# Three output projections of a four-layer kernel turned round: weights stationary, 256 tokens moving, then a copy and two transposes

## What is computed

```
L0_attn:  16 query heads of 64, rotary, causal;    out = o[tokens, 1024] @ Wo[1024, 128]
L1_attn:  16 query heads of 64, normalised q, k, mixed down to 8 x 64;  out = o[tokens, 512] @ Wout[512, 128]
L2_xattn: 16 heads of 64 over the 257 context rows; out = sum over heads h of  u_h[tokens, 128] @ M_h[128, 128]
```

## Time and profile before

| | |
|---|---|
| median of 3 runs | 7036.16 us (7031.7 to 7041.08) |
| span of the profiled execution, first to last instruction | 6974.0 us |
| median less span | 62.2 us |
| mean granted TensorE clock | 0.740 of 2.4 GHz |
| PE matmul busy | 5171.6 us (74%), 32012 records |
| PE weight load busy | 3702.6 us (53%) |
| DVE busy | 3139.9 us (45%) |
| ACT busy | 1901.3 us (27%) |

### The profile page before, as it was taken

How to read it: one execution, slowest core, us unless ns; L and a number is a source line. 1 busy time by engine, 2 the same in 40 slices (tenths; PEclk the granted TensorE clock), 3 DMA queues, 4 the chain that set the end, 5 groups by cost and what they waited for, 6 DMA issues and landing times.

```text
span 6974.0 us, 94942 instructions
## 1 busy us (share of the span) xinstructions
PE 5171.6 (74%) x32012; PEld 3702.6 (53%) x32012; DVE 3139.9 (45%) x8375; ACT 1901.3 (27%) x5099; POOL 660.4 (9%) x438
## 2 busy tenths in 40 slices
PE   6868687686876868768786686866778668786777
PEld 4545555465554655545554465544655446554455
DVE  3545335453444534445344543445434454444543
ACT  3223132232322323223132231422323223232231
POOL 1101011010200102001020010200102000020000
PEclk7758687696866968668686686867868578685777
DMA  3000000001000010000100001000000000000000
GB/s 116 1 1 1 32 10 1 1 1 37 4 1 1 1 37 5 1 1 1 37 4 1 1 1 39 3 1 1 13 27 3 1 1 13 27 3 1 1 1 2
DMA packets 17466, 74.76 MB, mean 11 GB/s; under 512 B 2106, under 2 KB 10298, under 8 KB 10436
## 3 DMA queue, kind: packets, MB, share of 16 engines
q1 hardware_dynamic: 16964, 68.29, 3.0%
HBM read 66.18 MB, written 2.10 MB: 10 GB/s over the span
## 4 chain that ended last, share of the span: by engine, by line
issue 82%; POOL 9%; PE 6%; DVE 2%; ACT 1%; POOLq 0%; DVEq 0%; ACTq 0%
POOL own L1196 3%; POOL big L1196 2%; POOL odd L1213 2%; POOL mid L1196 2%; POOL own L1201 1%; PE dveb L401 1%; PE actb L863 1%; PE oddb L873 0%; PE evenb L554 0%; PE dveb L704 0%; PE evenb L685 0%; PE oddb L554 0%; PE evenb L608 0%; PE oddb L677 0%; PE evenb L654 0%
## 5 line engine op out<-in xcount | busy, mean ns | idle before, releaser
L1196 POOL TENSOR_TENSOR own<-own,rinv 128x1028 f32<-128x1028 f32 x128 | 243.4, 1901 | 3045.0 <-DVE rinv L1665 3045.0
L935 ACT ACTIVATE lnv<-mv,wts 128x2 f32<-128x2 f32 x257 | 75.9, 295 | 1487.6 <-DVE mv L1348 1445.7
L393 PE MATMUL actb<-wts,xn 128*128 128x128 f32 x418 | 118.3, 385 | 474.9 <-DVE xn L1354 228.0
L942 ACT ACTIVATE PT<-actb 128x512 f32<-128x512 f32 (+2 forms) x576 | 314.1, 578 | 455.2 <-PE actb L642 151.2
L685 PE MATMUL evenb<-ctxT,big 128*128 128x257 f32 x1024 | 286.8, 404 | 127.2 <-ACT own L1098 115.2
L1098 ACT ACTIVATE own<-evenb,nmax 128x257 f32<-128x257 f32 x512 | 239.3, 473 | 424.6 <-DVE nmax L1651 424.6
L393 PEld LDWEIGHTS actb<-wts,xn 128*128 128x128 f32 x418 | 59.3, 188 | 531.4 <-issue 478.3
L1453 DVE CUSTOM_DVE_ANT_0 big<-evenb,own 128x257 f32<-128x257 f32 x512 | 198.8, 421 | 304.3 <-issue 303.7
L704 PE MATMUL dveb<-PT,ctx 128*128 128x512 f32 x512 | 263.8, 640 | 60.2 <-ACT PT L942 60.2
L685 PEld LDWEIGHTS evenb<-ctxT,big 128*128 128x128 f32 x1024 | 180.3, 196 | 234.8 <-ACT own L1098 166.5
L436 PE MATMUL evenb<-big 32*128 32x257 f32 x1024 | 237.4, 500 | 59.1 <-DVE nmax L1453 43.3
(11 more groups left out here) (350 smaller groups left out, 11639.1 us busy)
## 6 DMA issues: line engine op xcount, KB each, us to landing
ctxT<-in_ctxT SPq DMA_DIRECT2D x16, 1032.0 KB, 4.6
own<-in_fside SPq DMA_DIRECT2D x64, 257.0 KB, 7.8
ctx<-in_ctx SPq DMA_DIRECT2D x16, 1024.0 KB, 6.8
wts<-in_weights SPq DMA_DIRECT2D x1, 10592.0 KB
big<-in_fold SPq DMA_DIRECT2D x1, 2048.0 KB, 8.6
x<-in_x SPq DMA_DIRECT2D x16, 128.0 KB, 2.4
out<-xn SPq DMA_DIRECT2D x16, 128.0 KB, 1.9
mid<-in_ints SPq DMA_DIRECT2D x1, 576.0 KB
```

The source lines that it names most:

```text
L393: last = transpose(ps[:, 128 * t:128 * t + 128], xn[s][:, t, :], ident)
L942: op = activation(dst, ps[0:parts, 0:n], func or ACT.Copy, scale=scale)
L1196: nc.gpsimd.tensor_tensor(P[:, :, 0:SK], P[:, :, 0:SK], rinv[0][:, :].unsqueeze(2).to_broadcast((128, 4, SK)), ALU.mult).then_inc(*p_ready ...
```

## The change

The projections of a0, a1 and x2 go through `project_swapped`: weights stationary, all 256 tokens moving, one bank of aR with the output feature-major. ACT copies it to `oT[s]`; in a new stage `tokens_out` PE transposes the two halves back into a bank of dR, and DVE adds it as before. `STAGES` grows by one for `a0o`, `a1o` and `x2`.

```
-        STAGES = dict(... a0o=3, ... a1o=4, ... x2=2 * NB + 4, ...)
+        STAGES = dict(... a0o=4, ... a1o=5, ... x2=2 * NB + 5, ...)
...
+                def project_swapped(weights, tokens):
+                    ps = bank(aR, "yT")
+                    for j in range(len(weights)):
+                        last = mm(ps[:, 0:TOK], weights[j], tokens[j], start=(j == 0), stop=(j == len(weights) - 1))
+                    last.then_inc(*aR.filled.done)
+
+                def tokens_out():
+                    have(aR, "yT")
+                    ps = bank(dR, "out")
+                    for t in range(TG):
+                        last = transpose(ps[:, 128 * t:128 * t + 128], oT[s][:, 128 * t:128 * t + 128], ident)
+                    last.then_inc(*dR.filled.done)
...
-                    project_out([a0_o[:, j, :] for j in range(8)], [w("a0_Wo")[:, 128 * j:128 * j + 128] for j in range(8)])
+                    project_swapped([w("a0_Wo")[:, 128 * j:128 * j + 128] for j in range(8)], [a0_o[:, j, :] for j in range(8)])
+                    yield
+                    tokens_out()
...
-                    project_out([a1_o[:, j, :] for j in range(4)], [w("a1_Wout")[:, 128 * j:128 * j + 128] for j in range(4)])
+                    project_swapped([w("a1_Wout")[:, 128 * j:128 * j + 128] for j in range(4)], [a1_o[:, j, :] for j in range(4)])
+                    yield
+                    tokens_out()
...
-                    project_out([x2_q[:, :, h] for h in range(H)], [MU[:, 1, h, :] for h in range(H)])
+                    project_swapped([MU[:, 1, h, :] for h in range(H)], [x2_q[:, :, h] for h in range(H)])
+                    yield
+                    tokens_out()
...
+                    drain(oT[s][:, :], TOK)          # ACT: in a0o, a1o and x2, in the stage of the projection
+                    yield
...
+                    yield                            # DVE: add_out one stage later
                     add_out()
```

More of the change, by code:

```diff
@@ L47 @@
     xn_ready0=13, xn_ready1=13, s_ready0=5, s_ready1=5, e_ready0=6, e_ready1=6, p_ready0=21, p_ready1=21,
-    mix_ready0=10, mix_ready1=10, act_bank_filled=208, act_bank_drained=208, dve_bank_filled=160,
+    mix_ready0=10, mix_ready1=10, act_bank_filled=214, act_bank_drained=214, dve_bank_filled=160,
     dve_bank_drained=160, even_bank_filled=164, even_bank_drained=164, odd_bank_filled=68, odd_bank_drained=68)
@@ L276, in four_layers @@
             flags += [r.filled, r.drained]
-        STAGES = dict(ln=3, ln1x=3, ln1a=4, ln3a=4, x0=NB + 4, a0p=4, a0o=3, f0=4, x1p=3, x1o=3, a1p=3 * TG + 3, a1o=4, f1=2 + 2 * TG,
-                      x2=2 * NB + 4, a2=6, f2=2, x3=6, a3p=3, a3o=7, f3=3 + TG)
+        STAGES = dict(ln=3, ln1x=3, ln1a=4, ln3a=4, x0=NB + 4, a0p=4, a0o=4, f0=4, x1p=3, x1o=3, a1p=3 * TG + 3, a1o=5, f1=2 + 2 * TG,
+                      x2=2 * NB + 5, a2=6, f2=2, x3=6, a3p=3, a3o=7, f3=3 + TG)
         SUBLAYERS = [["ln", "x0"], ["ln", "a0p", "a0o"], ["ln", "f0"], ["ln1x", "x1p", "x1o"], ["ln1a", "a1p", "a1o"], ["ln", "f1"],
@@ L1081, in a1o @@
                     yield
+                    drain(oT[s][:, :], TOK)
+                    yield
                 def f1():
```

## The result

| | before | changed |
|---|---|---|
| median | 7033.93 us (7029.5 to 7041.08, 4 runs) | 7079.84 us (7077.05 to 7087.58, 4 runs) |
| ratio | | 1.0072 (1.0051 to 1.0092), 46 us slower |
| profiled span, clock | 6974.0 us, 0.740 | 7077.8 us, 0.737 |

The two profiled spans differ by 103.8 us and the medians by 46. That gap has to be understood before any step is judged. The changed kernel's profiled execution took 7079.61 us: only 1.8 us lie outside its span. So the 62.2 us between the median and the span of before weren't launch and ends. The profiled execution of before was itself some 60 us shorter than the timed ones.

A forecast was written before the change was run, and what follows sets the result against it. One chain hopping between engines in a merged order bounds the kernel. Steps sum to +8.2 us a trip, +66 us over 8 trips, on 7036.2: 7102, said as 7100 us; range for 8 in 10, 6985 to 7165.

The forecast's parts named there:

- The pace of the strided operand: x2 projection: strided moving columns pay as strided weights did, 13.8 us for 14.05, a gain of 0.25 us.
- the middle bound: x2 projection: moving operand read at the strided weights' 1.72 ns per column, about 13.8 us, between 6.9 and 27.5.
- The first rival: x2 projection: strided moving columns cost nothing extra, 6.9 us for 13.8, 110 us less, 6992 us; chance 0.16.
- the second: x2 projection: stride paid twice per column, 27.5 us, 219 us more, 7320 us; chance 0.08.
- The third: Projection as forecast, but the new order worth as much as it costs, -2 us a trip, 7020 us; chance 0.11.
- Step 7: End with x2 before the a2 projection: wait for DVE, then transposes, x2 addition later; +1.3 us a trip.
- Step 6: f1.5 after the x2 projection adds 4.6 us, f1.4 and f1.2 moves save 4.8; 0 a trip, -3 to +4.
- Step 5: a1 projection before f1.5, +3.0 us; farther up a1p.4 earlier, f1.2 and softmax waiting, +1.2; +4.2 a trip.
- Step 4: a1 projection waits for its input's eviction, two transposes, a1o.1 delays x1o.1; +2.2 us a trip.
- Step 2: f0.3 stands behind the a0 projection, so its matmuls and DVE work delay the addition; +1.5 us a trip.
- 0 saved: a0 and a1 projections: half the records, twice as wide, no matmul time saved; at most 0.4 us each.
- Step 1: Values of a0 fill PE's wait for POOL, a0's addition waits for DVE; -1 us a trip, -3 to +2.

The follow-up runs named there:

- e6: Changed kernel's stage order, projections in the old form without copy or transposes, each addition in its projection's stage; against before: 7078.88 us, 1.0060.
- e4: All three projections turned round, copy and transposes in the projection's own stage, old stage order; against before: 7002.82 us, 0.9957.
- e10: Changed kernel's stage order, projections in the old form, each in the last stage right before its addition; against before: 7036.71 us, 1.0079.
- e1: Only the x2 projection turned round, with its extra stage, a0 and a1 as before; against before: 7001.91 us, 0.9956.

## Why the prediction was right, point by point

**The pace of the strided operand: right.** 0.431 us per record forecast, 0.43 measured. The gain was forecast at 0.25 us; from the first record's start to the last one's end the projection of step 7 went from 14.24 to 14.05 us, that of step 6 from 14.03 to 14.14. The choice of the middle bound rested on ACT's drain paying as the weights did, and the layouts confirm that reading. The first rival fell on this, and the second. The third, an order worth as much as it costs, fell on steps 1, 5 and 6, none of which came out at its lower end.

**Step 7: tail right, +1.4 against +1.3.** The step as a whole grew by 0.2 to 0.3 only: in the fourth trip DVE's last combination now starts 63.5 us into the step where it was 64.6. The stages ahead of it moved too, which the sum had left out; which of them gains the 1.1 us isn't shown.

**Step 6: near, -0.8 against 0.** The tail grew from 15.6 (631.62 - 616.04) to 20.5 us (640.99 - 620.50), +4.9 against +4.6 forecast, so the gain ahead of it was 5.7 against 4.8.

**Step 5: the tail right (+3.3 against +3.0), the front too small (+3.3 against +1.2).** The mechanism that was named, that a1p.8 loses the cover of f1.3, is what the traces show. The term that was mis-sized is the value taken from its bounds of -3 to +4: it was drawn to the middle by the earlier L1571. That operation does start 6.3 us earlier (30.8 us into the step against 37.1), but DVE's f1.2, now behind the scores of a1, starts 4.5 us later (50.0 against 45.5), the reciprocal 2.4 us later, and at the end of the softmax, 66.1 us into the step, the two kernels are level, with f1.3 done before the change and still to do after it.

**Step 4: right in size, +1.9 against +2.2.** But the order without the turned-round form gives +0.3 in e6, and the form without the order +0.3 in e4. In e10 the step takes 95.6 us in one kind of trip and 97.8 in the other, with the same instructions, so the clock may be in the +1.9; that the terms named in the forecast make it up isn't shown.

**Step 2: +2.6 against +1.5.** Of the 1.1 us, the a0 projection is 1.0: its 16 records took 6.0 us from first start to last start where the 32 took 5.05, so "0 saved" was a loss there. The reason is the clock. Both start 43.4 us into the step at 1.2 GHz; the clock came back to 2.4 GHz 3.1 us into the projection before, and 5.5 us into it after the change. Stretches of the two projections, before and then changed:

```profile
2876.30:2881.50 5.20, 5.20 (x33) 5.10 (x32) 2.64 (x4) 0.00 (x0) 0.00 (x0) 0.70 0.00 0
```

```profile
2912.90:2919.20 6.30, 6.29 (x17) 5.07 (x18) 2.17 (x3) 0.00 (x0) 0.00 (x0) 0.56 0.00 0
```

**Step 1:** +1.1 against the short pattern, -1.0 against the long one, forecast -1; not decidable.

**The sum.** Forecast +8.2 us a trip. Against the short pattern it is 13.7: 11.1 in steps 2, 4, 5 where 7.9 were forecast, and +2.0 in step 8 that no step of mine had. Against the long pattern, which all four timed executions of before took beside the changed kernel, some 6 us.

**The base: wrong.** "The 62.2 us that the median has more than the span" was read as launch and ends. It was the clock: the profiled execution had the short pattern and the timed ones the long. Two errors of opposite sign met. The forecast loss was too small, by 3.5 us a trip in steps 1 to 7 and by the 2.0 us of step 8. And the base of 7036.2 already held some 7 us a trip of clock that before loses in its long pattern and the changed kernel for the most part does not; the 66 us, worked out on the short pattern, were added on top of it. That 7100 lies so near 7079.84 is luck. Beside a before in its short pattern, at 6983 us, the same 7080 would be 1.4% slower; that pair wasn't run side by side.

## What to carry to other kernels

Turning a matmul round moves a strided operand from the weight side to the moving side and pays the same; the layout, two neighbours in each 16 bytes, is what frees it, and only where the granted clock is full (0.22 against 0.43 us a record; at half the clock both took 0.43). Where every engine follows one merged list, an added stage is a reordering of the whole step: price first what DVE work lay under another engine's wait and where it goes. And compare the profiled execution's own time with its span before using a median as the base: here 1.8 us lay outside the span, and the other 60 of the 62.2 us were another execution, not overhead.

## What the hardware showed that was not expected

The same program ran in two patterns of granted clock, 0.728 to 0.736 and 0.740 to 0.745 on average, 7018 to 7047 us and 6970 to 6998 us, with the instructions of step 8 equal in both until the clock separates them (the executions are those of the kernel before). All 30 executions beside the first eight runs had the long one, nine of ten beside the last four the short one, though one of the earlier groups and the last were on the same chip. What chooses the pattern isn't settled. Small edits (e1, e4) left steps 9 to 11 and 0 as in the short pattern, while e10 alternated between two kinds of trip. The medians of e1 and e4, 33 and 32 us under before, come from that and not from work saved: both take 3.4 us a trip more than the short pattern.
